# Gather indices of an edge stream: one transfer for 32 tiles into three buffers, in place of one for 8 tiles into twelve

## The reference

```python
m = xl[src] + xr[dst] + e
score = jnp.where(m > 0, m, NEG_SLOPE * m) @ att
smax = jax.ops.segment_max(score, dst, num_segments=N)
es = jnp.exp(score - smax[dst])
denom = jax.ops.segment_sum(es, dst, num_segments=N)
alpha = es / (denom[dst] + 1e-16)
out = jax.ops.segment_sum(alpha[:, None] * xl[src], dst, num_segments=N)
```

## Time and profile before

| | us |
|---|---|
| median of three runs | 15,588.64 |
| lowest and highest run | 15,554.1 and 15,608.46 |
| span of the profiled execution | 15,438.3 |
| median above that span | 150.3 |

### The profile page before, as it was taken

One profiled execution on the slowest core, in us unless ns is written; L12 is line 12 of the kernel. 1 busy time (PEld: TensorE's weight loads), 2 busy tenths in 40 slices (PEclk: granted clock), 3 DMA queues, 4 the chain that ended last, 5 costly groups with the idle time before them and its releaser, 6 DMA issues. The chain is left out here.

```text
span 15438.3 us, 178521 instructions
## 1 busy us (share of the span) xinstructions
PE 7512.3 (49%) x38527; PEld 6783.9 (44%) x38528; DVE 6521.2 (42%) x11789; ACT 3580.5 (23%) x4864; POOL 7851.1 (51%) x8083
## 2 busy tenths in 40 slices
PE   0555555545555555355455554444444434545442
PEld 0544544544455544344444433444444334444442
DVE  3344444444444544333333343444444634434343
ACT  0222222212222222122222212222222122222220
POOL 3455555525555554356556615555455155555551
PEclk9566666656666666555555555555555555665565
DMA  2333333333333333222222233333333243333331
GB/s 69 76 78 80 78 75 76 78 62 80 76 78 78 80 78 62 41 46 47 47 45 49 47 101 82 76 75 78 74 76 76 73 117 83 85 83 85 83 74 22
DMA packets 1912984, 1106.77 MB, mean 72 GB/s; under 512 B 1548686, under 2 KB 1593762, under 8 KB 1911874
## 3 DMA queue, kind: packets, MB, share of 16 engines
q1 hardware_dynamic: 1654786, 718.42, 19.1%
q0 software_dynamic: 257568, 382.66, 12.6%
HBM read 1003.35 MB, written 96.52 MB: 71 GB/s over the span
## 5 line engine op out<-in xcount | busy, mean ns | idle before, releaser
L1006 POOL DMA_INDIRECT ds_gat<-table_d,ds_idx x1568 | 1508.6, 962 | 1562.1 <-issue 803.9
L1006 POOL DMA_INDIRECT as_gat<-table_a,as_idx x1568 | 1529.5, 975 | 1254.5 <-DMA as_idx<-in_srcT 721.1
L1006 POOL DMA_INDIRECT bs_gat<-table_b,bs_idx x1568 | 1538.6, 981 | 1199.0 <-DMA bs_idx<-idx_d 680.0
L1006 POOL DMA_INDIRECT es_gat<-table_e,es_idx x1568 | 1523.7, 972 | 1195.7 <-issue 578.3
L1006 POOL DMA_INDIRECT cs_gat<-table_c,cs_idx x1568 | 1532.7, 978 | 1088.9 <-issue 544.8
L1271 PE MATMUL cs_psA<-cs_ahot,cs_wtd 128*68 128x128 f32 x3136 | 670.8, 400 | 434.0 <-ACT cs_psA L1031 315.3
L1271 PE MATMUL es_psA<-es_ahot,es_wtd 128*68 128x128 f32 x3136 | 619.2, 377 | 406.5 <-ACT es_psA L1031 256.1
L1271 PE MATMUL bs_psA<-bs_ahot,bs_wtd 128*65 128x128 f32 x3136 | 624.2, 361 | 393.8 <-issue 351.3
L1271 PEld LDWEIGHTS cs_psA<-cs_ahot,cs_wtd 128*68 128x68 f32 x3136 | 605.2, 221 | 456.0 <-issue 455.6
L1256 PE MATMUL es_psM<-es_dst,es_hot 128*128 128x64 f32 x3136 | 595.2, 361 | 415.1 <-issue 202.3
L1256 PEld LDWEIGHTS es_psM<-es_dst,es_hot 128*128 128x128 f32 x3136 | 568.7, 275 | 462.2 <-issue 369.8
(11 more groups left out here) (734 smaller groups left out, 16292.6 us busy)
## 6 DMA issues: line engine op xcount, KB each, us to landing
ds_dst<-dst_d SPq DMA_DIRECT2D x1568, 34.0 KB
as_rank<-rel_d SPq DMA_DIRECT2D x196, 256.0 KB
as_dst<-dst_a SPq DMA_DIRECT2D x1568, 32.0 KB
as_ea<-in_eaT SPq DMA_DIRECT2D x196, 256.0 KB
bs_rank<-rel_d SPq DMA_DIRECT2D x196, 256.0 KB
bs_dst<-dst_b SPq DMA_DIRECT2D x1568, 32.0 KB
bs_ea<-in_eaT SPq DMA_DIRECT2D x196, 256.0 KB
cs_rank<-rel_d SPq DMA_DIRECT2D x196, 256.0 KB
```

Of the source, the lines that this page charges most:

```text
L1006: g_.indirect_dma_start(gat[s][:, j, :], None, table, bass.IndirectOffsetOnAxis(ap=idxS[s][:, j:j + 1].bitcast(U32), axis=0)).then_inc(got ...
```

## The change

The index buffers idxS become three, each of 128 x 32 int32, one for a chunk. SP loads a chunk's indices in one transfer when it comes to the chunk's first group, after a wait for the landing of the gathers of all four groups that read the buffer three chunks before. In the other three groups of a chunk SP has no index transfer and no such wait. POOL waits for the indices at a chunk's first group only, and its gathers read eight columns of the chunk's buffer. The wait for `weighted` stays at every group. Line numbers behind the edit move by two or three: the index load is L973, rank L975, dst L979, masks L985 and L986, the gather L1009.

```diff
--- before.py
+++ after.py
@@ -888,7 +888,7 @@
             return stage_sem(nc, ctx, nm + name)
 
         gat = [sb(f"gat{s}", [P, GROUP, row]) for s in range(RING)]
-        idxS = [sb(f"idx{s}", [P, GROUP], I32) for s in range(RING)]
+        idxS = [sb(f"idx{s}", [P, CT], I32) for s in range(3)]
         rank = [sb(f"rank{s}", [P, GE], BF16) for s in range(4)]
         dsts = [sb(f"dst{s}", [P, GROUP, dc]) for s in range(4)]
         hot = [sb(f"hot{s}", [P, GE]) for s in range(2)]
@@ -926,7 +926,7 @@
         psX, psI = ps("psX"), ps("psI")
 
         fed = [sem(f"fed{s}") for s in range(4)]
-        idxd = [sem(f"idxd{s}") for s in range(RING)]
+        idxd = [sem(f"idxd{s}") for s in range(3)]
         got = [sem(f"got{s}") for s in range(RING)]
         masked = [sem(f"masked{s}") for s in range(3)]
         dsted = [sem(f"dsted{s}") for s in range(4)]
@@ -967,8 +967,10 @@
                 def feed(it, s):
                     g = it * RING + s
                     c = it * 3 + s // CG
-                    wait(sp, got[s], it * GOT)
-                    sp.dma_start(idxS[s][:, :], idx[:, bass.ds(g * GROUP, GROUP)]).then_inc(idxd[s], 16)
+                    if s % CG == 0:
+                        for e in range(CG):
+                            wait(sp, got[s + e], it * GOT)
+                        sp.dma_start(idxS[s // CG][:, :], idx[:, bass.ds(c * CT, CT)]).then_inc(idxd[s // CG], 16)
                     wait(sp, hots, g - 3)
                     sp.dma_start(rank[s % 4][:, :], relrow[:, bass.ds(g * GE, GE)].broadcast_to([P, GE])).then_inc(fed[s % 4], 16)
                     bases = load_windows(nc, m["base"], g * GROUP, GROUP, mybir.EngineType.SP, RANKS - 1)
@@ -999,12 +1001,13 @@
             def _(g_):
                 def gather(it, s):
                     g = it * RING + s
-                    g_.wait_ge(idxd[s], it * 16 + 16)
+                    if s % CG == 0:
+                        g_.wait_ge(idxd[s // CG], it * 16 + 16)
                     wait(g_, weighted, g - RING + 1)
                     g_.sem_inc(pch, 1)
                     for j in range(GROUP):
                         g_.indirect_dma_start(gat[s][:, j, :], None, table,
-                                              bass.IndirectOffsetOnAxis(ap=idxS[s][:, j:j + 1].bitcast(U32), axis=0)).then_inc(got[s], 16)
+                                              bass.IndirectOffsetOnAxis(ap=idxS[s // CG][:, s % CG * GROUP + j:s % CG * GROUP + j + 1].bitcast(U32), axis=0)).then_inc(got[s], 16)
                 rounds(g_, gather, GROUPS)
 
             @block.scalar
```

## The result

The changed kernel takes 16,545.1 us (median of five runs, 16,500.0 to 16,572.8) beside 15,588.6 us for the kernel before on the same chip: a ratio of 1.061, 95% interval 1.059 to 1.063. It is slower by 6%. Its profiled execution has a span of 16,567.6 us.

What follows compares the result with a forecast made beforehand. No engine was busy over 51%; POOL's index waits, really waits for SP, bound it. Terms of +127 (cs), +284 (es), -78 (as, bs) and -39 us (ds) gave +294 on 15,588.6: 15,880 us, range 15,100 to 16,400.

Steps and rivals of the forecast that it cites:

- What bounds the kernel: All streams: waits, not busy engines; POOL's index wait is for SP, and all other engines slow in POOL's long runs.
- The removed transfers: SP's queue: three of four index transfers go, saving 0 to 1.6 us per chunk; 1.6 taken in cs and es, half elsewhere.
- the terms for SP: SP's savings: 0.4 us per group in cs and es, 78 us in as and bs together, 39 us in ds.
- The larger transfer and the added wait: Index load on SP: 128 bytes a partition in place of 32, and the wait for earlier gathers; both were to cost nothing.
- The price of a run of four: cs and es: four groups without a pause slow the others, +0.65 and +1.45 us per group, +127 and +284 us.
- the stops in as and bs: POOL in as and bs: three groups, a stop for weighing, one more; only SP's half saving is left, -78 us.
- the rival that all four streams run four groups: as, bs, cs, es: as and bs also lose 1.05 us per group, +412 us in place of -78; 16,370 us, chance 17%.
- ds: Stream ds: the weighing on DVE is the limit and stays it; -39 us, no move by more than 1%.
- Landings: Rival for as, bs, cs, es: long runs cost nothing, each index wait removed saves about 2 us; -500 us, 15,090 us, chance 20%.
- The +235 us for as and bs at the upper end: as and bs: upper end of their term, if one of two chunks ran through four groups like cs.

Runs made afterwards that it cites:

- e1_brake: Kernel after, chunk load kept, but POOL waits at a chunk's groups 1 to 3 for a count SP raises where the old index transfer stood; 0.987 of the kernel before.
- e6_lag1: Kernel after, POOL waiting before each group until the gathers of the group just before have landed; 0.909 of the kernel before.
- e8_drain_by8: Kernel before (index transfer per group), POOL waiting behind each group's eight gathers until they have landed; 0.911 of the kernel before.
- e10_pause4: Kernel after with four small POOL fills behind the eighth gather of each group, no wait for landings; 0.884 of the kernel before.
- e16_pause4_by8: Kernel before (index transfer per group) with four small POOL fills behind each group's eight gathers; 0.886 of the kernel before.
- e3_early: Kernel before with twelve buffers and one index transfer per group, each sent four groups earlier by SP; 1.011 of the kernel before.
- e4_drain: Kernel after, POOL waiting behind each group's eight gathers until they have landed; 0.924 of the kernel before.

## Why the prediction was wrong

It forecast 15,880 us, slower by 1.9%; it is slower by 6.1%, and 16,545 us lie above the range. By its steps:

- **What bounds the kernel** was right: POOL's wait for indices is a wait for SP, and SP and PE are slowed in POOL's runs (the prediction had all other engines slowed; DVE, its measure of work, mostly waits for PE). So was the direction: the index wait was a brake, and without it the kernel is slower (e1_brake).
- **The removed transfers** at up to 1.6 us a chunk: where POOL is braked much as before, e1_brake gains 1.3% (some 200 us, where the terms for SP came to 274), and part of that is landings; where POOL sets the time the load by the chunk gains 0.2% (e6_lag1 beside e8_drain_by8) or nothing clear of noise (e10_pause4 beside e16_pause4_by8). **The larger transfer and the added wait** cost nothing, as said (e16_pause4_by8 beside e10_pause4).
- **The price of a run of four** was right: 56.4 to 60.1 us forecast for a cycle in cs, 585.5 / 10 = 58.6 measured. There is luck in it: the first two tens gave DVE more than forecast (4.84 and 1.72 us beside 3.80 and 1.01), the third and fourth less (0.39 and 0.27, forecast 0.99 each). But I charged it against 13.5 us per group, worked out, and not against the 13.0 that the trace has. From first to last gather cs has 14.4 us per group now; it gave +264 us where I had +127. By 13.0 it would have been +225. In es it is +230, where I had +284 against a worked-out 12.5 us per group; by the trace's 13.3 that would have been +127, so its nearness is luck.
- **The step that failed is the stops in as and bs.** I had three groups, a stop for weighing and one more there, no dearer than two and two: -78 us. All 49 runs of as and of bs are of four groups, and these streams gave +276 and +293 us (569 in place of -78), more than half of the loss. The rows below are the streams of the kernel after from first to last gather: us, then busy us and numbers of PE, PEld, DVE, ACT and POOL, then PEclk, DMA share and GB/s. Before they took 2,702, 2,669, 2,553, 2,912 and 2,606 us. The profile of the kernel before, with its 15,438 us, lies with the chips on which it takes 15,409 to 15,428 us, so about 1%, 130 us, of the sum of 1,091 should be the chip's; the rest agrees with the 956 us between the medians.

```profile
480.60:3459.50 2978.90, 1385.53 (x7825) 1240.28 (x7825) 1223.47 (x2198) 670.94 (x843) 1505.52 (x1568) 0.61 0.32 70
3683.50:6646.10 2962.60, 1379.83 (x7832) 1232.90 (x7832) 1212.81 (x2020) 674.36 (x847) 1512.25 (x1568) 0.61 0.32 70
6896.40:9713.90 2817.50, 1201.81 (x6313) 1145.65 (x6313) 802.42 (x1638) 667.64 (x847) 1510.77 (x1568) 0.55 0.24 43
10049.50:12992.30 2942.80, 1352.17 (x6560) 1203.33 (x6561) 1236.74 (x2491) 673.50 (x851) 1507.98 (x1568) 0.57 0.32 76
13279.60:16116.50 2836.90, 1127.58 (x6298) 1039.62 (x6298) 1024.41 (x1826) 670.17 (x846) 1506.73 (x1568) 0.60 0.33 77
```

The room that POOL has at a run's start was read from the kernel before, where the idle stretches of as are 8 us on the mean (21 now), and from one start in as the earlier trace rows. Counted over all 100 starts in as behind the first twelve groups, that trace has a room of g+1 at 57, g at 1, and g+2 or g+3 at 42, so already there one start was not enough to tell. In the longer idle stretch of the changed kernel DVE catches up by one group more. At the start of the run at 1330.47 448 gathers are out, 56 groups, and 47 are weighed, so groups up to 58 may go, g+2 and not g+1:

```profile
L1009 POOL DMA_INDIRECT as_gat<-table_a,as_idx x448: 942/947/1437, 480.6 to 1308.4; - x150
...
L1164 DVE TENSOR_TENSOR as_wtd<-as_gat,as_alpha x47: 679/691/702, 598.1 to 1323.4; 128x520 f32<-128x520 f32 x47
```

DVE weighs two more before the fourth group is due (49 by 1340.6), and POOL runs through. At 41 of 46 starts in as the room is g+2 now, at the others g+3. In cs and es, where I had four in a row everywhere, 13 and 15 of the 49 chunks are cut into one and three by the weighing. It was the other way around, and the rival that all four streams run four groups (16,370 us, 17%) comes nearest to what happened.
- **ds** moved by 30 us, 1.0%, about what the chips differ; that it hangs on the weighing was right.
- **Landings**, the rival on the faster side at 20%: refuted by the result, since its longer runs were to cost nothing, and by e3_early, where most index waits go and nothing is won. By the Trainium skill's "DMA: Bandwidth & Descriptors", section "Rules for kernel authors", many small transfers made into one should win; with the slowing out of the way the runs show 0.2% of it at most (e6_lag1 beside e8_drain_by8).
- The range left out the upper end because I gave that rival no room beyond 16,400; its own sum of 1.05 us per group was too low, too (+1.4 in as, +1.5 in bs, +1.3 in cs, +1.2 in es, before the 1% of the chip). The +235 us for as and bs at the upper end does not follow from the terms given.

## What to carry to other kernels

A wait that costs hundreds of us may be what keeps a producer from running its neighbours down: before removing it, see what they do in the stretch that it would lengthen. When a feedback loop sets run lengths, read slack in the state that the change makes, not in the one it leaves. And where indirect gathers from GpSimd run beside engines that issue many small instructions, as SP and PE do here, try pacing them: four small fills behind every eight gathers made this kernel 11.5% faster, with either way of loading the indices.

## What the runs showed of the hardware that was not expected

- Beside indirect gathers of 128 rows that POOL issues every 1.25 us the issue on SP and PE is slow after some ten us, to the point that eight DMA issues take 23.5 us and not 4, and PE's matmuls come 2.8 us apart, while the DMA engines are busy for 0.20 of the fourth ten us of a run. At 1.46 us per gather, on the mean, they keep up. A limit this sharp (ratio 0.958 at 11.34 us per eight, 0.884 at 11.66) was not expected, nor that a thinner stream with no more than 1.12 us between two gathers does the same as pauses.
- With eight gathers out POOL went on 2.4 us after its last one ended, when it waited for all to land (e4_drain).
- A fill of 0.33 us behind a gather moved the next one by only 0.19 us (1.25 to 1.44), since 0.30 us lie between two gathers anyway; four in a row, 1.09 us, moved it by 1.58 us (0.30 to 1.88), since the next group waits for the last fill's count.
